# Taking out the small weight loads that TensorE ran behind VectorE, and pairing the evictions of a weight merge

## The chip, the cores and the metric

One Trainium2 chip, all 8 cores. Each core runs the same program on one batch element of 2048 positions and 1024 features, and no data passes between cores. The metric is the device time of the slowest core in microseconds.

## The reference, cut to what matters

Two layers on x of shape (8, 2048, 1024):

```python
x = x + minGRU(layernorm(x))            # gates by sigmoid, a scan over time, layernorm, residual
h = layernorm(x) @ fakequant8(W_fc).T + 2 * lora   # 1024 -> 4096
x = x + (gelu(h) @ fakequant8(W_proj).T + 2 * lora)  # 4096 -> 1024
# layer 1
xk, xv, xr = blends of layernorm(x) with itself shifted by one position
k, v, sr = xk @ Wk.T, xv @ Wv.T, sigmoid(xr @ Wr.T)
x = x + (sr * wkv(w, u, k, v)) @ Wo.T   # wkv: a running weighted mean over time
x = x + tanh(layernorm(x) @ W @ A1 @ A2 + bias)
```

`fakequant8` scales a weight by its largest magnitude over 127, rounds it and scales it back. The kernel folds the low-rank part into the rounded weight.

## The kernel before

Activations lie with features on the 128 partitions (8 groups, `kk` or `m`) and positions along the free dimension (2048, in tiles of 512, or in two halves `th` of 1024). The program is written stage by stage with small bodies, `k.T` for TensorE, `k.V` for VectorE, `k.S` for ScalarE, `k.G` for GpSimd and `k.Y` for the SyncE queue. `k.dep` notes what a body has to wait for, and `body` writes those waits in front of it. Every engine works through its bodies in the order in which the Python code emits them, so a wait in front of one body holds back all later bodies of that engine.

`warm()` emits a TensorE body of two weight loads of the tile `ONESB`, whose result nothing uses. In front of it stands a wait for the newest VectorE mark at that place in the program. It is called at eight places.

The stages that the change touches, in order:

1. **Combine.** `cmb` forms the new residual for 8 groups by 4 tiles, with `warm()` after each tile. Then come `ln_stats` (VectorE casts and squares, TensorE sums over partitions) and `xh2_v`/`xh2_g`, the normalised input of the feed-forward part, with `warm()` after each of six groups.
2. **Rounding W_fc.** `pass2(WFCT, ...)` takes 32 chunks of 128x1024. `qv` is four VectorE instructions a chunk, and `warm()` follows each. Only after all 32 does the code emit the merges: `merge_chunk(..., "s")`, for each half chunk one small matmul (`asl` by `bgr`, the low-rank part), one by the identity `IDN`, and the ScalarE body `mev` that copies the sum over the rounded weight. The low-rank operand comes in by `aring`, two slots loaded by GpSimd's queue. The banks go round over four.
3. **Rounding W_proj.** `pass2(WPRT, ...)`, again 32 chunks of `qv` with `warm()` after each, reading through `ring2` and writing into the tile `H`.
4. **Feed-forward.** Four position tiles `tt`. In each, `mfc` (8 groups `g` of 32 matmuls, read out by the ScalarE body `efc` with GELU), then `mpr` (2 groups of 128 matmuls) and `epr`. For `tt == 0` the merges of W_proj stand between the two: `merge_chunk(..., "v")` with the matmul body `abm2` and the VectorE body `mev2`. So `mfc` of the first tile is emitted after all `warm()` calls of step 3, and `mpr` after all `mev2`.
5. **Blends and wkv.** For each half `th`: eight blends (`bl_g` on GpSimd, `bl_v` on VectorE) with `warm()` after each. Then for each group `m`: `mkv` (32 matmuls for k and v into banks a to a+3), `mr` (16 matmuls for r into banks b and b+1, b = 4 - a, a alternating 0 and 4), `ev1a` and `ev1b` (ScalarE, two exponentials of k), `warm()`, `ev2` (ScalarE, exponential of r), `v1` (VectorE: products, two scans, numerator and denominator), `warm()`, `sdiv` (ScalarE: logarithm and exponential), `v2` (VectorE, last product), `warm()`. `EKBp` and `EKUp` have two buffers each; `EWB`, `EKV` and `DEN` have one.
6. **Output projection.** `mwo` (16 matmuls), `awo` on VectorE, with residual tiles coming in by `x2ring` and going out by `owr`, both on the SyncE queue.
7. **Last part.** `ln_stream_stats`, then `xh4` for 16 tiles (two halves `h2` of 8 groups; every fourth on GpSimd) with `warm()` after each. Then `mm1` (16 matmuls, two banks) and `em1` (VectorE) for 2 halves by 8 groups, and `mm2` and `mm3` in the same way.

Of the kernel before, what the change touches and what calls it, by code (L numbers as in the profile page):

```python
# [8 lines left out]
AF = mybir.ActivationFunctionType  # L9
# [122 lines left out]
def _ap(t):  # L132
    return t if isinstance(t, bass.AP) else t[:]


def bc16(t):
    return _ap(t).bitcast(BF16)
# [6 lines left out]
def tmax(*toks):  # L144
    at = {}
    for t in toks:
        if t is None:
            continue
        if isinstance(t, dict):
            for p, v in t.items():  # L150
                at[p] = max(at.get(p, 0), v)
        else:
            at[t[0]] = max(at.get(t[0], 0), t[1])
    return at
# [27 lines left out]
def build(T=2048, debug=False):  # L182
# [33 lines left out]
    XB0 = nc.alloc_sbuf_tensor("XB0", [128, 8 * RT], BF16)  # L216
# [7 lines left out]
    ONESB = nc.alloc_sbuf_tensor("ONESB", [128, 128], BF16)  # L224
# [16 lines left out]
    PB = [nc.alloc_psum_tensor(f"PB{i}", [128, NSZ], F32) for i in range(8)]  # L241

    with nc.Block() as blk:
        k = K(nc, blk)
# [14 lines left out]
        def bank_wait(ctx, idxs):  # L259
            for i in idxs:  # L260
                if banks[i] is not None:
                    ctx.wait(*banks[i])

        WRHS = bc16(_ap(XB0))[:, 0:512]

        def warm():
            at = {"vector": k.ch["vector"].val}
            k.dep(["tensor"], at=at)
            def wf(t):
                t.ldweights(ONESB[:])  # L270
                t.ldweights(ONESB[:])
            k.T(wf)

        def gdma(wn, out, in_, gate=None, **kw):
            c = k.ch["gd_" + wn]
# [424 lines left out]
        for m in range(8):  # L700
            for n in range(NT):
                sl = slice(n * NSZ, (n + 1) * NSZ)
                if m < 6:
                    sch = "spx%d%d" % (2 * (m // 2), 2 * (m // 2) + 1)
                    slot, tok = xring.load(ci, SP1[m * 128:(m + 1) * 128, sl],
                                           gates=[(sch, 32)])
                else:
                    slot, tok = Xr[m][:, sl], None
                eng = "vector" if ci % 4 != 3 else "gpsimd"
                if eng == "vector":  # L710
                    k.dep([eng], at=tmax(lnh_rows, scan_done[m], tok))
                    def cmb(e, m=m, sl=sl, slot=slot):
                        tmp = SCR[2]
                        e.tensor_sub(tmp[:], HD[m][:, sl], EX[0][:, sl])
                        e.chain()
                        e.tensor_mul(tmp[:], tmp[:], EX[1][:, sl])
                        e.chain()
                        e.tensor_scalar(tmp[:], tmp[:], SM[:, 16 + m:17 + m],
                                        SM[:, 24 + m:25 + m], OP.mult, OP.add)
                        e.chain()  # L720
                        e.tensor_add(tmp[:], tmp[:], XBF[m][:, sl])
                        e.chain()
                        e.tensor_add(Hr[m][:, sl], tmp[:], slot)
                        comb_done[(m, n)] = (eng, e.mark())
                    k.V(cmb)
                else:
                    k.dep([eng], at=tmax(lnh_rows, scan_done[m], tok))
                    def cmb_g1(e, m=m, sl=sl):
                        tmp = SCR[3]
                        e.tensor_sub(tmp[:], HD[m][:, sl], EX[0][:, sl])  # L730
                        e.chain()
                        e.tensor_mul(tmp[:], tmp[:], EX[1][:, sl])
                        e.mark()
                    k.G(cmb_g1)
                    k.dep(["vector"], ["gpsimd"])
                    def cmb_s(e, m=m):
                        e.tensor_scalar(SCR[3][:], SCR[3][:],
                                        SM[:, 16 + m:17 + m],
                                        SM[:, 24 + m:25 + m],
                                        OP.mult, OP.add)  # L740
                        e.mark()
                    k.V(cmb_s)
                    k.dep(["gpsimd"], ["vector"])
                    def cmb_g2(e, m=m, n=n, sl=sl, slot=slot):
                        tmp = SCR[3]
                        e.tensor_add(tmp[:], tmp[:], XBF[m][:, sl])
                        e.chain()
                        e.tensor_add(Hr[m][:, sl], tmp[:], slot)
                        comb_done[(m, n)] = ("gpsimd", e.mark())
                    k.G(cmb_g2)  # L750
                if m < 6:
                    xring.release(ci, comb_done[(m, n)])
                    ci += 1
                warm()
        comb_m = {m: tmax(*(comb_done[(m, n)] for n in range(NT)))
                  for m in range(8)}

# [11 lines left out]
        ln2_rows = ln_stats(lambda kk, n: Hr[kk][:, n * NSZ:(n + 1) * NSZ],  # L769
                            lambda kk, n: comb_done[(kk, n)], EX[0], EX[1])  # L770
        xh2_tok = {}
        for kk in (0, 1, 2, 4, 5, 6):
            k.dep(["vector"], at=tmax(ln2_rows) if kk == 0 else None)
            def xh2_v(v, kk=kk):
                for n in range(NT):
                    sl = slice(n * NSZ, (n + 1) * NSZ)
                    v.tensor_sub(SCR[2][:], Hr[kk][:, sl], EX[0][:, sl])
                    v.chain()
                    v.tensor_mul(XBF[kk][:, sl], SCR[2][:], EX[1][:, sl])
                    v.chain()  # L780
                xh2_tok[kk] = ("vector", k.ch["vector"].val)
            k.V(xh2_v)
            warm()
        k.dep(["gpsimd"], at=tmax(ln2_rows))
        def xh2_g(g):
            for kk in (3, 7):
                for n in range(NT):
# [50 lines left out]
                     ["ar0", "ar1"], issue_eng="gpsimd")  # L838
        ali = [0]

        def merge_chunk(kk, c, dst, bs_ap, a_hbm, qv_tok, first, evac,
                        bs_tok, merged):
            asl, atok = aring.load(ali[0],
                                   a_hbm[0:16, kk * 128:(kk + 1) * 128])
            for h in range(2):
                b = abk[0] % 4
                abk[0] += 1
                dgr = dst(kk, c)[:, h * 512:(h + 1) * 512]
                bgr = bs_ap[0:16, c * 1024 + h * 512:c * 1024 + (h + 1) * 512]
                at = tmax(qv_tok, atok,  # L850
                          *([bs_tok, ("gd_idn", 16)] if first[0] else []))
                first[0] = False
                if evac == "s":
                    k.dep(["tensor"], at=at)
                    def abm(t, b=b, dgr=dgr, bgr=bgr, asl=asl):
                        bank_wait(t, [b])
                        t.matmul(PB[b][:], asl, bgr, start=True, stop=False)
                        t.matmul(PB[b][:], IDN[:], dgr, start=False,
                                 stop=True)
                        t.mark()  # L860
                    k.T(abm)
                    k.dep(["scalar"], ["tensor"])
                    def mev(s, b=b, dgr=dgr):
                        s.activation(dgr, PB[b][:], AF.Copy)
                        banks[b] = ("scalar", s.mark())
                    k.S(mev)
                    merged[(kk, 2 * c + h)] = ("scalar", k.snap("scalar"))
                else:
                    k.dep(["tensor"], at=at)
                    def abm2(t, b=b, bgr=bgr, asl=asl):  # L870
                        bank_wait(t, [b])
                        t.matmul(PB[b][:], asl, bgr, start=True, stop=True)
                        t.mark()
                    k.T(abm2)
                    k.dep(["vector"], ["tensor"])
                    def mev2(v, b=b, dgr=dgr):
                        v.scalar_tensor_tensor(dgr, PB[b][:], 1.0,
                                               dgr, OP.mult, OP.add)
                        banks[b] = ("vector", v.mark())
                    k.V(mev2)  # L880
                    merged[(kk, 2 * c + h)] = ("vector", k.snap("vector"))
            aring.release(ali[0], ("tensor", k.snap("tensor")))
            ali[0] += 1

        def pass2(hbm, order, dst, gates, qtok, qcol, ring, ring_i0, iq,
                  deferred):
            for i, (kk, c) in enumerate(order):
# [19 lines left out]
                qv_tok = ("vector", k.snap("vector"))  # L907
                ring.release(ring_i0 + i, qv_tok)
                deferred.append((kk, c, qv_tok))
                warm()  # L910

        fcm_ready = {}
        fc_first = [True]
# [177 lines left out]
        for th in range(2):  # L1091
            hsl = slice(th * TH, (th + 1) * TH)
            for kk in range(KT):
# [42 lines left out]
                btok = ("vector", k.snap("vector"))  # L1136
                qring.release(kk % 2, btok)
                xhb_free[kk % 2] = btok
                warm()
            blends_done = ("vector", k.snap("vector"))  # L1140

            for m in range(8):
# [51 lines left out]
                    for i in range(NHH):  # L1194
                        banks[a + i] = tok
                k.S(ev1b)
                warm()
                eku_tok = ("scalar", k.snap("scalar"))
                k.dep(["scalar"], at=tmax(rh_done[(th, m)], prev(v1_done, 1)))
                def ev2(s, m=m, b=b):  # L1200
# [49 lines left out]
                                           OP.add, OP.mult)  # L1250
                    v1_done[(th, m)] = ("vector", v.mark())
                k.V(v1)
                warm()
                k.dep(["scalar"], at=tmax(v1_done[(th, m)]))
                def sdiv(s):
                    s.activation(EWB[:], EKV[:], AF.Ln)
# [14 lines left out]
                    g1_done[(th, m)] = tok  # L1271
                    rw_done[(th, m)] = tok
                k.V(v2)
                warm()

        mloop_v = ("vector", k.snap("vector"))
        mloop_s = ("scalar", k.snap("scalar"))
# [99 lines left out]
        for h2 in range(NCH):  # L1377
            for kk in range(KT):
# [12 lines left out]
                qring.release(li4, tok2)  # L1391
                xh4_tok[(kk, h2)] = tok2
                li4 += 1
                warm()

        def h1_sl(kk):
            return bc16(Hf[kk // 2])[:, (kk % 2) * T:(kk % 2) * T + T]
# [200 lines left out]
```

How the kernel before makes its waits and increments, by code:

```python
    def mark(self):  # L47
        K = self._K
        c = K.ch[self._n]
        assert self.last is not None, "mark with no pending instruction"
        self.last.then_inc(c.sem, 1)
        c.val += 1
        self.last = None
        return c.val
# [1 line left out]
    def chain(self):  # L56
        v = self.mark()
        self._e.wait_ge(self._K.ch[self._n].sem, v)
# [1 line left out]
    def wait(self, name, val):  # L60
        if val > 0:
            self._e.wait_ge(self._K.ch[name].sem, val)
# [1 line left out]
    def dma(self, name, out, in_, **kw):  # L64
        K = self._K
        c = K.ch[name]
        ins = self._e.dma_start(out=out, in_=in_, **kw)
        ins.then_inc(c.sem, 16)
        c.val += 16
        self.last = None
        return c.val
# [34 lines left out]
        def run(eng):  # L106
            ctx = Eng(self, eng, name)
            pend = self.pend[name]
            own = self.ch[name]
            if own.val > pend.get(name, 0):
                pend[name] = own.val
            if pend:
                for p, v in sorted(pend.items()):
                    if v > 0:
                        eng.wait_ge(self.ch[p].sem, v)
                pend.clear()
            fn(ctx)
            if ctx.last is not None:
                ctx.mark()
# [159 lines left out]
            def f(g):  # L279
                ins = g.dma_start(out=out, in_=in_, **kw)
                ins.then_inc(c.sem, 16)
                g.last = None
# [1255 lines left out]
        def fin(y):  # L1538
            for name, v in sorted(fin_vals.items()):
                if v > 0:
                    y.wait_ge(k.ch[name].sem, v)
```

## Time and profile before

| | us |
|---|---|
| runs shown, timed | 3179.94 and 3232.47, median 3206.21 |
| the profiled execution | 3165.46 |
| its span on the slowest core (core 7) | 3163.9 |
| spans of the eight cores | 3129.1 to 3163.9 |
| TensorE matmul busy | 1348.0 (43%) |
| VectorE busy | 1461.9 (46%) |
| ScalarE busy | 653.1 (21%) |

No engine is busy for even half of the span. The time is made of stages with different limits, and of waits between engines. So the busy shares are read stage by stage, and each stage's rows for what ended the idle time. A row of the timeline gives the start and the duration in us, the engine, the operation with output<-input, and in brackets the idle time before it with what ended it. PEld is TensorE's weight load.

### The profile page before, as it was taken

Reading aid. Unit: us, or ns where it says so; the run is one execution under the profiler, and the core shown is the slowest. Engines: PE = TensorE matmul, PEld = TensorE weight load, DVE = VectorE, ACT = ScalarE, POOL = GpSimd, SP = SyncE. Lnnn points to the kernel's source line nnn. Section 1 sums busy time; section 2 is a strip of 40 time slices with the busy share of each in tenths; the row PEclk is TensorE's granted clock in tenths of the full one; section 3 lists DMA queues with packets and bytes.
Section 4 is the critical chain, followed back from the end, with each engine's and each line's share of the span. In section 5 each row is a group of like instructions: output and inputs, shape, how many; then the busy total and the mean of one; then the engine's idle time right before and its main releaser. Section 6 shows DMA issues by size and latency. Waiting matters only on the chain.

```text
span 3163.9 us, 19191 instructions; the slowest of 8 cores (3129.1 to 3163.9 us)
## 1 busy us (share of the span) xinstructions
PE 1348.0 (43%) x4868; PEld 509.3 (16%) x5232; DVE 1461.9 (46%) x1702; ACT 653.1 (21%) x754; POOL 274.7 (9%) x219
## 2 busy tenths in 40 slices
PE   3054433040005387797976311433043345240885
PEld 0021110000001132333332000111011111000332
DVE  3866668888999813100101376233824321006322
ACT  0033320000009540223130001233032310070013
POOL 0300000303001001000000024000400000041000
PEclk9987765555555586999988555776566676655998
DMA  7223320400333200201104711000100024652015
GB/s 174 80 89 122 120 82 24 144 32 2 106 108 108 96 1 2 53 21 34 38 17 84 158 50 36 0 0 0 40 0 0 0 50 94 119 150 87 13 42 165
DMA packets 73846, 201.00 MB, mean 64 GB/s; under 512 B 9440, under 2 KB 9440, under 8 KB 70928
## 3 DMA queue, kind: packets, MB, share of 16 engines
q1 hardware_dynamic: 59952, 165.76, 17.3%
q0 software_dynamic: 11776, 19.34, 4.2%
q10 hardware_dynamic: 2016, 14.68, 1.2%
q8 instruction: 47, 0.77, 0.1%
q14 instruction: 55, 0.45, 0.1%
HBM read 179.24 MB, written 39.85 MB: 69 GB/s over the span
## 4 chain that ended last, share of the span: by engine, by line
DVE 34%; PE 28%; DMA 17%; ACT 9%; issue 8%; POOL 2%; SPq 1%; DVEq 1%; ACTq 0%; PEld 0%; POOLq 0%; PEldq 0%
PE PB L38 28%; DVE X L38 9%; DVE SC L38 8%; DMA SC<-SP 7%; DVE E L38 7%; DMA E<-SP 4%; DVE AT L38 4%; ACT L38 4%; DVE XB L38 3%; DVE H L38 2%; DMA E<-WPRT 2%; DVE MX L38 2%; ACT SC L38 2%; ACT X L38 2%; DMA SMT<-SM 1%
## 5 line engine op out<-in xcount | busy, mean ns | idle before, releaser
L38 ACT ACT_TABLE_LOAD x249 | 319.5, 1283 | 2494.5 <-PE PB L38 1190.6
L38 PE MATMUL PB<-XB,X 128*128 128x512 bf16 x1280 | 292.9, 387 | 179.4 <-PE L38 119.0
L38 PE MATMUL PB<-X,H 128*128 128x512 bf16 x512 | 153.7, 473 | 491.1 <-PE L38 491.1
L38 PE MATMUL PB<-XB,H 128*128 128x512 bf16 x896 | 230.1, 416 | 262.2 <-DVE X L38 145.8
L38 PE MATMUL PB<-E,H 128*128 128x512 bf16 x1152 | 279.6, 408 | 63.1 <-DVE X L38 44.7
L38 DVE TENSOR_SCALAR AT<-PB,QS,SMT 128x512 f32<-128x512 f32 x32 | 25.9, 810 | 468.7 <-PE PB L38 342.9
L38 PE MATMUL PB<-SC,ONESB 128*128 128x512 bf16 x256 | 129.5, 608 | 167.7 <-DVE SC L38 145.4
L38 PEld LDWEIGHTS <-ONESB 128*128 128x128 bf16 x364 | 27.2, 103 | 994.7 <-issue 994.7
L38 PE MATMUL PB<-E,ASL 16*128 16x512 bf16 x64 | 37.1, 580 | 291.9 <-DVE AT L38 243.3
L38 PEld LDWEIGHTS PB<-XB,X 128*128 128x128 bf16 x1280 | 123.8, 99 | 229.8 <-issue 95.1
L38 PEld LDWEIGHTS PB<-E,H 128*128 128x128 bf16 x1152 | 118.3, 104 | 224.4 <-issue 108.6
L38 PEld LDWEIGHTS PB<-XB,H 128*128 128x128 bf16 x896 | 90.2, 105 | 382.2 <-issue 305.6
L38 DVE TENSOR_SCALAR SC<-E,DRV 128x1024 f32<-128x1024 f32 x16 | 12.1, 753 | 296.1 <-ACT SC L38 296.1
L38 PE MATMUL PB<-H,X 128*128 128x512 bf16 x512 | 120.8, 391 | 30.3 <-ACT X L38 20.8
L38 DVE TENSOR_TENSOR X<-PB,SC 128x512 f32<-128x512 f32 x32 | 22.1, 692 | 185.9 <-DMA SC<-SP 178.7
L38 ACT ACTIVATE E<-PB,SMT,QS 128x512 bf16<-128x512 f32 x128 | 89.2, 777 | 0.4
L38 POOL TENSOR_TENSOR E<-E 128x1024 f32<-128x1024 f32 x28 | 78.7, 2812 | 94.6 <-DMA E<-SP 92.1
L38 DVE SCALAR_TENSOR_TENSOR H<-PB,H 128x512 bf16<-128x512 f32 x64 | 44.3, 692 | 89.0 <-PE PB L38 88.5
L38 PE MATMUL PB<-MX,SC 1*128 1x1 f32 x4 | 1.1, 343 | 195.8 <-DVE SC L38 195.8
L38 DVE CAST H<-PB 128x512 bf16<-128x512 f32 x64 | 41.2, 686 | 90.7 <-PE PB L38 90.7
L38 PEld LDWEIGHTS PB<-X,H 128*128 128x128 bf16 x512 | 58.5, 116 | 98.7 <-issue 65.7
L38 DVE RECIPROCAL E<-SC 128x512 f32<-128x512 f32 x20 | 67.0, 3352 | 2.4 <-DVE SC L38 0.5
(137 smaller groups left out, 1919.4 us busy)
## 6 DMA issues: line engine op xcount, KB each, us to landing
AT<-WFCT SPq DMA_DIRECT2D x32, 512.0 KB, 3.4
E<-WFCT SPq DMA_DIRECT2D x32, 512.0 KB, 3.4
SC<-WPRT SPq DMA_DIRECT2D x32, 512.0 KB, 3.3
SC<-SP SPq DMA_DIRECT2D x64, 256.0 KB, 3.6
E<-SP SPq DMA_DIRECT2D x56, 256.0 KB, 4.2
AT<-SP SPq DMA_DIRECT2D x24, 512.0 KB, 3.7
E<-SP SPq DMA_DIRECT2D x24, 512.0 KB, 3.7
X<-XT SPq DMA_DIRECT2D x2, 4096.0 KB, 30.0
```

What stands on the lines that cost most here:

```text
L38: ins = f(*args, **kw)
```

## The change

The function `warm` and all its calls are gone, eight call sites in the code. The six bodies of `xh2_v` become one. In `merge_chunk` with `"s"` the ScalarE body is emitted once for both halves of a chunk: it waits for both halves' matmuls, does the two copies, and frees both banks with one mark. All else is as before: each engine's other bodies stand in the same order.

```diff
-        def warm():
-            at = {"vector": k.ch["vector"].val}
-            k.dep(["tensor"], at=at)
-            def wf(t):
-                t.ldweights(ONESB[:])
-                t.ldweights(ONESB[:])
-            k.T(wf)
...
@@ combine @@
                     xring.release(ci, comb_done[(m, n)])
                     ci += 1
-                warm()
...
@@ xh2 @@
-        for kk in (0, 1, 2, 4, 5, 6):
-            k.dep(["vector"], at=tmax(ln2_rows) if kk == 0 else None)
-            def xh2_v(v, kk=kk):
+        k.dep(["vector", "gpsimd"], at=tmax(ln2_rows))
+        def xh2_v(v):
+            for kk in (0, 1, 2, 4, 5, 6):
...
-            k.V(xh2_v)
-            warm()
-        k.dep(["gpsimd"], at=tmax(ln2_rows))
+        k.V(xh2_v)
...
@@ merge_chunk @@
-                    k.dep(["scalar"], ["tensor"])
-                    def mev(s, b=b, dgr=dgr):
-                        s.activation(dgr, PB[b][:], AF.Copy)
-                        banks[b] = ("scalar", s.mark())
-                    k.S(mev)
-                    merged[(kk, 2 * c + h)] = ("scalar", k.snap("scalar"))
+                    sgr.append((b, dgr, kk, 2 * c + h))
+                    if h == 1:
+                        k.dep(["scalar"], ["tensor"])
+                        def mev(s, pair=tuple(sgr)):
+                            for b2, d2, _, _ in pair:
+                                s.activation(d2, PB[b2][:], AF.Copy)
+                            tok = ("scalar", s.mark())
+                            for b2, _, _, _ in pair:
+                                banks[b2] = tok
+                        k.S(mev)
+                        stok = ("scalar", k.snap("scalar"))
+                        for _, _, kk2, g2 in sgr:
+                            merged[(kk2, g2)] = stok
+                        del sgr[:]
...
@@ pass2, after each chunk @@
                 deferred.append((kk, c, qv_tok))
-                warm()
...
@@ blends @@
                 xhb_free[kk % 2] = btok
-                warm()
...
@@ wkv, in the loop over m @@
                 k.S(ev1b)
-                warm()
...
                 k.V(v1)
-                warm()
...
                 k.V(v2)
-                warm()
...
@@ xh4 @@
                 li4 += 1
-                warm()
```

## Rows read from the trace of the kernel before

**Rows 1.** Page, the chain that ended last, share of the span by engine.
```profile
DVE 34%; PE 28%; DMA 17%; ACT 9%; issue 8%; POOL 2%; SPq 1%; DVEq 1%; ACTq 0%; PEld 0%; POOLq 0%; PEldq 0%
```

**Rows 2.** Windows: stretch, length, busy and count per engine, granted clock, DMA share, GB/s.
```profile
785.50:942.90 157.40, 0.00 (x0) 4.73 (x64) 143.57 (x128) 7.42 (x4) 2.05 (x4) 0.50 0.32 108
942.90:1100.70 157.80, 71.61 (x128) 17.83 (x192) 143.57 (x129) 120.34 (x128) 16.96 (x32) 0.50 0.31 103
...
1295.00:1760.00 465.00, 347.97 (x1531) 150.49 (x1529) 40.55 (x54) 97.67 (x120) 5.99 (x8) 0.89 0.21 44
...
2930.00:3160.00 230.00, 179.26 (x767) 72.92 (x765) 63.03 (x96) 40.79 (x48) 4.00 (x2) 0.95 0.23 69
```

**Rows 3.** Timeline, end of rounding W_fc, first merge.
```profile
943.02 0.15 PEld L38 LDWEIGHTS <-ONESB 128*128 128x128 bf16 x2 [4.82 <-issue]
...
943.77 0.58 PE L38 MATMUL PB<-E,ASL 16*128 16x512 bf16 x1 [239.85 <-DVE AT L38]
```

**Rows 4.** Timeline, ScalarE during the merges of W_fc, two later half chunks.
```profile
1064.30 1.28 ACT L38 ACT_TABLE_LOAD   x1
...
1065.60 0.60 ACT L38 ACTIVATE X<-PB 128x512 bf16<-128x512 f32 x1
...
1066.33 1.28 ACT L38 ACT_TABLE_LOAD   x1
```

**Rows 5.** Timeline, end of rounding W_proj, first feed-forward tile, its merges.
```profile
1100.72 0.15 PEld L38 LDWEIGHTS <-ONESB 128*128 128x128 bf16 x2 [4.77 <-issue]
...
1101.64 4.78 PE L38 MATMUL PB<-XB,X 128*128 128x512 bf16 x11 [34.19 <-PE L38]
...
1157.36 7.07 PE L38 MATMUL PB<-XB,X 128*128 128x512 bf16 x32 [0.57 <-PE PB L38]
...
1165.34 3.08 DVE L38 SCALAR_TENSOR_TENSOR H<-PB,H 128x512 bf16<-128x512 f32 x4 [64.73 <-PE PB L38]
```

**Rows 6.** Timeline, wkv loop, one group m from its `v1` on.
```profile
2098.12 0.75 DVE L38 TENSOR_SCALAR SC<-E,DRV 128x1024 f32<-128x1024 f32 x1 [18.48 <-ACT SC L38]
...
2100.17 4.47 DVE L38 TENSOR_TENSOR_SCAN X<-SC,X 128x1024 f32<-128x1024 f32 x2
...
2109.21 1.28 ACT L38 ACT_TABLE_LOAD   x1 [11.27 <-DVE X L38]
...
2112.88 1.23 DVE L38 TENSOR_TENSOR XB<-X,SC 128x1024 bf16<-128x1024 f32 x1 [3.75 <-ACT SC L38]
...
2115.05 9.48 PE L38 MATMUL PB<-X,H 128*128 128x512 bf16 x32 [20.85 <-PE L38]
...
2124.67 1.28 ACT L38 ACT_TABLE_LOAD   x1 [11.96 <-PE PB L38]
```

**Rows 7.** Waits, first half of the wkv loop: total us, times, longest us.
```profile
ACT L38 <- PE PB L38: 176.8, 8, 92.2
```

**Rows 8.** Timeline, first stage (165 to 470 us), VectorE's scan beside matmuls.
```profile
190.69 4.42 DVE L38 TENSOR_TENSOR_SCAN H<-X 128x2048 f32<-128x2048 f32 x1
193.08 3.61 PE L38 MATMUL PB<-XB,H 128*128 128x512 bf16 x16 [0.37 <-PE PB L38]
```

**Rows 9.** Timeline, start of the output projection, and a later matmul group after a pause.
```profile
2559.74 0.32 SPq L67 DMA_DIRECT2D SC<-SP  x1
...
2568.22 0.69 DVE L38 TENSOR_TENSOR X<-PB,SC 128x512 f32<-128x512 f32 x1 [7.16 <-PE PB L38]
...
2587.75 5.21 PE L38 MATMUL PB<-XB,H 128*128 128x512 bf16 x16 [8.61 <-DVE X L38]
```

**Rows 10.** Page, DMA issues: queue, count, KB each, median us to landing.
```profile
SC<-SP SPq DMA_DIRECT2D x64, 256.0 KB, 3.6
```

**Rows 11.** Timeline, end of the last normalisation and start of the last part.
```profile
2926.68 1.23 DVE L38 TENSOR_TENSOR XB<-AT,E 128x1024 bf16<-128x1024 f32 x1
...
2938.67 3.61 PE L38 MATMUL PB<-XB,X 128*128 128x512 bf16 x16 [0.37 <-PE PB L38]
```

**Rows 12.** Timeline, `xh2`: the same product beside GpSimd's products.
```profile
734.63 1.56 DVE L38 TENSOR_TENSOR XB<-SC,E 128x512 bf16<-128x512 f32 x1
```

More of the change, by code:

```diff
@@ L262, in bank_wait @@
                     ctx.wait(*banks[i])
-        WRHS = bc16(_ap(XB0))[:, 0:512]
-        def warm():
-            at = {"vector": k.ch["vector"].val}
-            k.dep(["tensor"], at=at)
-            def wf(t):
-                t.ldweights(ONESB[:])
-                t.ldweights(ONESB[:])
-            k.T(wf)
         def gdma(wn, out, in_, gate=None, **kw):
@@ L839, in build @@
         ali = [0]
+        sgr = []
         def merge_chunk(kk, c, dst, bs_ap, a_hbm, qv_tok, first, evac,
```

## The prediction

> **What bounds the kernel now.** I read the page first: by its busy shares (in the table above) no engine is busy for half the span, and the chain that ended last passes through VectorE, TensorE, transfers and ScalarE in turn [rows 1]. The limit is therefore order. I then took the windows by stage and, at every place where `warm()` stands, the timeline, asking one question: what stands behind this wait in TensorE's queue, and was it ready earlier?
>
> Three stretches show the answer. While W_fc is rounded, VectorE is busy 143.57 of 157.40 us and TensorE runs nothing but the 64 idle loads; while W_proj is rounded, VectorE is busy just as long, and TensorE only does the merges [rows 2]. Then VectorE idles for 64.73 us while TensorE does the first feed-forward tile [rows 5]. The first merge matmul starts at 943.77, right behind the last idle load of the W_fc rounding, although the first chunk was rounded some 150 us before [rows 3]. The first feed-forward matmul starts at 1101.64, behind the last idle load of the W_proj rounding [rows 5], although it needs no W_proj.
>
> In the wkv loop one turn is a closed ring: matmuls of k and v, exponentials, `v1`, `sdiv`, `v2`, and only then, behind the third `warm()`, the next matmuls [rows 6]. Nothing overlaps there.
>
> **The change, part by part.** The matmuls keep their order; what goes is the wait for VectorE in front of them.
>
> *A. Feed-forward, first tile.* VectorE has one unbroken queue here: 32 chunks of W_fc and 32 of W_proj, 785.5 to 1100.6 [rows 2, 5]. The change takes nothing from it. What moves is TensorE's work beneath it. One chunk is rounded every 4.92 us (157.4/32). A merge needs per chunk four small matmuls and two ScalarE copies. On ScalarE a half chunk took 2.02 us, of which 1.28 is a table load, once per body [rows 4]. Paired, a chunk takes about 1.28 + 2 x 0.60 + 0.1 = 2.6 us in place of 4.0, and either is below 4.92. So the merges keep up with the rounding and end about 7 us after the last chunk, near 950. The pairing saves 32 table loads, 41 us of ScalarE time, at no gain on the path: the rounding covers it. Without that cover it would be worth up to 32 x 1.4 = 45 us.
>
> `mfc` of the first tile then runs from about 950 for as long as now, 1101.64 to about 1164.5, 63 us. It ends near 1013, under the W_proj rounding. At 1100.6 the first `mev2` finds its banks filled and starts about 0.3 us later, in place of at 1165.34, which had waited 64.73 us [rows 5]. Gain 64.4 us. The merges of W_proj after it are paced by `mev2` and by the loads of `ASL`, and keep their length. What is late next is those same merges: the loss of the whole overlap would give back 64.4, and that is the far bound of this term. The near bound is 0 loss: there are 88 us of slack (1101 - 1013).
>
> *B. The wkv loop.* In the new order, `mkv` of group m+1 needs its banks: b and b+1 are freed by `ev2` of m, and b+2 and b+3 were freed by `v1` of m-1. So it starts about when `v1` of m does. From there, `v1` lasts 11.1 us (2098.12 to 2109.2), `sdiv` until about 2112.7, thus 14.6 us [rows 6]. `mkv` needs 9.5 [rows 6] and `mr`, 16 matmuls at full rate, 0.4 + 3.6 [rows 8], together 13.5, and `mkv` is what `ev1a` needs. So `ev1a` of m+1 finds its input ready and follows `sdiv` in ScalarE's queue after about 0.1 us. Before, ScalarE idled 11.96 us there, waiting for TensorE [rows 6]. Of the 16 turns, 14 follow another turn; the two first of a half wait for the blends as before. In the first half the wait came 8 times for 176.8 us, of which the first was 92.2, so the other seven had 12.09 each [rows 7]. Gain 14 x (12.09 - 0.1) = 168 us. The turn goes from 34.3 to about 22.4: `v1` 11.1, `sdiv` 3.5, the three exponential bodies the rest, and `v2` (1.23) lies under the exponentials.
>
> What is late next is ScalarE and VectorE, in series; TensorE has about 8.7 us to spare. Its clock: the matmuls of a turn begin at 1.2 GHz (the 32 take 9.48 [rows 6], where 32 at 2.4 GHz took 7.07 [rows 5]). A pause of 8.61 us elsewhere was also followed by a slow start, 5.21 for 16 in place of 3.61 [rows 8, 9], so I take the same slow start. If all 48 ran at 1.2 GHz, at 4.78/11 = 0.43 us each [rows 5], `mkv` would end after 13.8, still in time, and `mr` after 21.0, where `ev2` wants it at 22.4 less its own 2.5 (a table load of 1.28 and two copies of 0.60, as in [rows 4]), 19.9. That costs 1.1 a turn, 16 us in all: the far bound.
>
> Does VectorE slow down when TensorE works beside it? Two scans of 1024 with TensorE idle took 4.47 [rows 6], one scan of 2048 beside matmuls at full rate 4.42 [rows 8]. I take 0.
>
> *C. Output projection.* The first two `mwo` run under the last `v1`. `awo` then waits for the first residual tile, issued at 2559.74. Such a transfer lands 3.6 us after its issue in the median [rows 10], so it starts near 2563.5 in place of 2568.22 [rows 9]: 4.7 us, bounds 0 and 7.2 (the whole wait on TensorE). After it the stage goes at the pace of its transfers, as now.
>
> *D. Last part.* `mm1` of the first two groups runs under the second half of `xh4`. The third needs a bank that `em1` frees. `em1` can begin when VectorE's last `xh4` ends (2926.68 + 1.23), so the third group starts near 2929.5 in place of 2938.67 [rows 11]. It starts slow, 1.6 us more [rows 8, 9]. Gain 7.6 us, bounds 0 and 9.
>
> *E. The rest.* The combine, `xh2` and the blends are paced by VectorE and GpSimd, and nothing useful stood behind the waits there. The idle loads in front of the first matmuls of a half took under 1 us each: 1 us in all. Joining the `xh2` bodies saves nothing that counts.
>
> **Two rules weighed.** The granted clock is 0.50, the level of 1.2 GHz, while only the 64 idle loads run [rows 2], so they hold nothing up, and the turn's matmuls start slow right behind them [rows 6]. The Trainium skill, "TensorE: Matmul & The Clock Gate", "Why this matters for your kernels", asks that TensorE have no idle gaps, since the clock falls back in them. If the idle loads counted as work for it, taking them out would cost; by the rows it costs nothing, and I go by the rows. Second, the wait in front of an idle load did hold the merges [rows 3]. The same page ("Step-by-step: what each phase is for") says that only weight loads are pulled ahead, and matmuls keep program order; had the merges been able to pass the waiting loads, the change would do nothing. The trace agrees with the page.
>
> **Sum.** 64.4 + 168 + 4.7 + 7.6 + 1 = 245.7, or 246 us. The profiled execution took 3165.5, so the same kind of execution would take 2920. The runs shown lie higher, 3179.94 and 3232.47. I take off the sum from 3179.94, the middle one of the three times: 2934 us. Against the median of the two runs shown, 3206, the sum would give 2960.
>
> **Rivals.**
> - *TensorE late in the wkv loop:* all its matmuls there at 1.2 GHz, 16 us back, 2950. For it: the slow starts. Against: the clock rose within every burst. Chance 0.05.
> - *A does not come:* something else holds the first feed-forward tile to the end of the W_proj rounding, for example a merge paced below the rounding. 2934 + 64 = 2998. Against: both paces above. Chance 0.03.
> - *B does not come:* another wait closes the ring, of a bank or of a single buffer. 2934 + 168 = 3102. I find none in the code. Chance 0.03.
> - *Contention:* VectorE slows beside TensorE as it does beside GpSimd, where a product of 128x512 took 1.56 [rows 12] in place of 0.69 ([rows 9] has an addition of that size). On the 11 us of `v1` that would add up to 14 us a turn, 196 in all, 3130. Against: the scans. Chance 0.02.
> - *The change does nothing:* 3180. Against: the waits in [rows 3, 5]. Chance 0.02.
> - *Slower: the clock.* The idle loads keep the clock ready in a way that the granted clock does not show, and without them long bursts stay at 1.2 GHz. In the feed-forward stretch from 1295 to 1760, 1531 matmuls took 348 us and would take 658 at 0.43 each; in the last part, 767 took 179 and would take 330 [rows 2, 5]. Together 461 lost against 246 won: 2934 + 461 = 3395. It decides once 53% of these matmuls stay slow. Against: the clock is 0.50 with the loads [rows 2], and the feed-forward stretch, at 0.89, has none in it. Chance 0.02.
>
> My forecast keeps 0.83.
>
> **How the numbers follow.** 2934 is the likeliest case. Upward the range takes in the late TensorE, the higher starting time (3232 - 246 = 2986) and the loss of A: 3000. Downward it takes the lowest starting time (2920) and 25 us for terms B to D being under-counted: 2895. Faster by over 2% (below 3142; about what a measurement of this kernel can tell from no change) are the forecast and the first four rivals, with 0.95 after rounding down; within 2% the case of no effect, 0.03; slower 0.02.
>
> **What would show each step.** A: merge matmuls among the rounding from 790 on, feed-forward matmuls before 1100, and no VectorE pause of 64 us. B: about 22.4 us between one `v1` and the next, and ScalarE without its 12 us wait on TensorE. If instead the wait stays and names a bank, B is wrong; if `v1` grows beyond 11.1, it is contention; if ScalarE waits on TensorE for `ev2`, it is the clock. C and D: first `awo` and third `mm1` 4 to 9 us sooner against the end of the stage before. The clock: if the steady 7.1 us per 32 matmuls of the feed-forward tiles rises, the slow rival holds.

## The result, and the profile after

The changed kernel takes 2919 us where the kernel before took 3164 (medians of the comparison's runs); the ratio is 0.9214, with a 95% interval of 0.9187 to 0.9242. Some executions of either kernel take some per cent longer, with a lower granted clock on one die, and the ratios leave them out. The runs of before came out lower in this comparison than in the two shown earlier, so the 2934 that was forecast is 15 us high, while the saving, 245 us between the medians, is the 246 of the sum. In the two profiled executions the spans are 3163.9 and 2916.6 us: 247.3 less.

The page after, in the same order as before: busy time by engine, and the chain that ended last.

```profile
PE 1350.7 (46%) x4868; PEld 483.4 (17%) x4868; DVE 1463.9 (50%) x1702; ACT 609.0 (21%) x722; POOL 273.9 (9%) x219
...
DVE 37%; PE 23%; DMA 19%; ACT 9%; issue 8%; POOL 1%; SPq 1%; DVEq 1%; ACTq 0%; POOLq 0%
```

TensorE and VectorE do the same work in the same time as before: 4868 matmuls and 1350 us, 1702 instructions and 1464 us. 364 weight loads are gone, and 32 ScalarE table loads. TensorE's share of the chain fell from 28% to 23% [rows 1]. The time came out of waiting.

**The feed-forward part.** Windows of core 5 of the changed kernel, in the columns of [rows 2]: rounding W_fc, rounding W_proj, merges of W_proj.

```profile
788.10:945.30 157.20, 69.38 (x124) 12.55 (x124) 142.33 (x127) 80.36 (x97) 17.09 (x35) 0.50 0.34 109
945.30:1104.80 159.50, 62.11 (x264) 25.61 (x264) 144.90 (x130) 35.46 (x45) 1.45 (x3) 0.69 0.32 101
1104.80:1171.30 66.50, 34.78 (x60) 5.97 (x60) 44.17 (x64) 0.00 (x0) 13.56 (x28) 0.50 0.03 2
```

VectorE is as busy as before in both roundings. TensorE now does the merges in the first and the first feed-forward tile in the second. Timeline of the same kernel: the first merge, the first feed-forward matmuls, the last 32 of that first tile, the last rounding instruction and the first `mev2`.

```profile
797.85 0.58 PE L38 MATMUL PB<-E,ASL 16*128 16x512 bf16 x1 [91.07 <-ACT E L38]
...
952.26 8.06 PE L38 MATMUL PB<-XB,X 128*128 128x512 bf16 x29 [2.71 <-ACT X L38]
...
1007.44 7.07 PE L38 MATMUL PB<-XB,X 128*128 128x512 bf16 x32 [0.57 <-PE PB L38]
...
1103.37 1.23 DVE L38 SCALAR_TENSOR_TENSOR H<-SC,AT 128x1024 bf16<-128x1024 f32 x1
1104.69 7.85 DVE L38 SCALAR_TENSOR_TENSOR H<-PB,H 128x512 bf16<-128x512 f32 x10
```

The merge starts 9.7 us after the rounding of its chunk began (788.17), released by ScalarE, which had scaled its low-rank operand. The first feed-forward matmul starts at 952.26, and the first tile ends at 1014.5. The first `mev2` follows the last rounding instruction after 0.09 us, where it waited 64.73 us before [rows 5].

**The wkv loop.** Timeline of one turn, from `v1` to the next `v1`, to be laid beside [rows 6].

```profile
2007.14 0.75 DVE L38 TENSOR_SCALAR SC<-E,DRV 128x1024 f32<-128x1024 f32 x1 [6.83 <-ACT SC L38]
2007.46 8.47 PE L38 MATMUL PB<-X,H 128*128 128x512 bf16 x32 [9.06 <-ACT SC L38]
...
2009.19 4.47 DVE L38 TENSOR_TENSOR_SCAN X<-SC,X 128x1024 f32<-128x1024 f32 x2
...
2016.29 3.61 PE L38 MATMUL PB<-XB,H 128*128 128x512 bf16 x16 [0.37 <-PE PB L38]
...
2017.90 1.28 ACT L38 ACT_TABLE_LOAD   x1 [10.94 <-DVE X L38]
...
2021.58 1.22 DVE L38 TENSOR_TENSOR XB<-X,SC 128x1024 bf16<-128x1024 f32 x1 [3.75 <-ACT SC L38]
2021.59 1.28 ACT L38 ACT_TABLE_LOAD   x1 [0.18 <-ACT SC L38]
...
2024.05 1.28 ACT L38 ACT_TABLE_LOAD   x1
...
2026.80 1.28 ACT L38 ACT_TABLE_LOAD   x1 [0.19 <-ACT X L38]
...
2029.35 0.75 DVE L38 TENSOR_SCALAR SC<-E,DRV 128x1024 f32<-128x1024 f32 x1 [6.55 <-ACT SC L38]
```

The matmuls of the next group start 0.3 us after `v1`, released by ScalarE (`ev2`, which frees their banks), and end at 2015.9 for k and v, before the ScalarE body that reads them starts at 2021.6, and at 2019.9 for r, before its body starts at 2026.8. The exponentials follow the end of `sdiv` at once: 0.18 us of idle time where it had been 11.96 [rows 6]. The turn is 22.2 us (2029.35 - 2007.14). Over all 14 turns that follow another turn, the mean from one `v1` to the next is 22.2 us, where it was 34.2. The scans take 4.47 us with matmuls beside them, as without. The clock still starts low: 32 matmuls took 8.47 us where 7.07 is full rate [rows 5].

**Output projection and last part.** The first `awo`, and then the third and fourth `mm1`, to be laid beside [rows 9] and [rows 11].

```profile
2329.16 0.69 DVE L38 TENSOR_TENSOR X<-PB,SC 128x512 f32<-128x512 f32 x1 [2.00 <-DMA SC<-SP]
```

```profile
2685.68 5.52 PE L38 MATMUL PB<-XB,X 128*128 128x512 bf16 x16 [18.14 <-DVE H L38]
2691.57 3.61 PE L38 MATMUL PB<-XB,X 128*128 128x512 bf16 x16 [0.37 <-PE PB L38]
```

The first `awo` now waits 2.00 us, for its residual tile, and no longer for TensorE. The third `mm1` starts 1.7 us after the last `xh4` of VectorE (which ends at 2684.03), with a slow start: 5.52 us for 16 matmuls in place of 3.61.

**Where the 247 us went,** between the same marks in both timelines:

| stretch | before | after | difference | forecast |
|---|---|---|---|---|
| start to first rounding | 785.6 | 788.2 | +2.6 | 0 |
| first rounding to first `mev2` | 379.7 | 316.5 | -63.2 | -64.4 |
| first `mev2` to first wkv matmul | 778.6 | 773.4 | -5.2 | -1 |
| wkv loops, to the end of the last `v2` | 617.1 | 449.1 | -168.0 | -168 |
| last `v2` to first `awo` | 7.2 | 2.0 | -5.2 | -4.7 |
| first `awo` to the last `xh4` of VectorE | 359.7 | 354.9 | -4.8 | 0 |
| last `xh4` to the fourth `mm1` | 14.7 | 7.5 | -7.2 | -7.6 |
| fourth `mm1` to the end | 221.3 | 225.0 | +3.8 | 0 |

The four stretches with a forecast of 0 or -1 moved by -5 to +4 us, -3.6 in all. Their causes were not traced. Moves of this size can't be told from the spread between executions: in the traces of the experiments below whose code up to there is that of the changed kernel, the first rounding starts anywhere from 780.8 to 793.4 us.

### The profile page after: what moved, and what is told of

Its sections match the earlier page's. It is cut to its first block, busy times and chain, and to the rows that moved or that the text cites. A ratio compares the mean times of both kernels' runs of the same rounds, so it can differ in the third digit from the quotient of the medians.

```text
span 2916.6 us, 18362 instructions; the slowest of 8 cores (2889.4 to 2916.6 us)
## 1 busy us (share of the span) xinstructions
PE 1350.7 (46%) x4868; PEld 483.4 (17%) x4868; DVE 1463.9 (50%) x1702; ACT 609.0 (21%) x722; POOL 273.9 (9%) x219
## 4 chain that ended last, share of the span: by engine, by line
DVE 37%; PE 23%; DMA 19%; ACT 9%; issue 8%; POOL 1%; SPq 1%; DVEq 1%; ACTq 0%; POOLq 0%
PE PB L38 23%; DVE SC L38 9%; DVE X L38 9%; DMA SC<-SP 7%; DVE E L38 7%; DVE AT L38 4%; ACT L38 4%; DMA E<-SP 4%; DVE XB L38 3%; DVE H L38 3%; DMA E<-WPRT 2%; DVE MX L38 2%; ACT SC L38 2%; ACT X L38 2%; DMA SMT<-SM 1%
## 5 line engine op out<-in xcount | busy, mean ns | idle before, releaser
L38 PE MATMUL PB<-E,H 128*128 128x512 bf16 x1152 | 279.0, 408 | 63.2 <-DVE X L38 44.6
L38 PE MATMUL PB<-SC,ASL 16*128 16x512 bf16 x64 | 36.5, 570 | 118.7 <-DVE H L38 90.3
L38 PE MATMUL PB<-XB,ONESB 128*128 128x512 bf16 x64 | 32.4, 608 | 78.8 <-POOL XB L38 45.8
```

The costliest lines, as they stand in the source:

```text
L38: ins = f(*args, **kw)
```

## The experiments

Each ratio is to the kernel before on the same chip, which took 3167 to 3178 us (median) there. All kernels but the first start from the changed one, 2919 us.

### The loads stay, the wait goes

```diff
         def warm():
-            at = {"vector": k.ch["vector"].val}
-            k.dep(["tensor"], at=at)
             def wf(t):
```

> The kernel before with the wait for VectorE taken out of warm(), and nothing else: all 364 idle weight loads stay, and the merges stay unpaired. Theory (only the wait cost time): the whole gain is there, about 2920 us, ratio near 0.922, within 10 us of the changed kernel; the loads themselves cost at most 364 x 0.15 = 55 us of TensorE time, nearly all beside other work, so at most some 5 us. Rival (the loads themselves held the matmuls up, or the pairing carried the gain): 3000 us or more. Second rival (loads do hold the clock up once they no longer block): granted clock above 0.50 while W_fc is rounded.

Measured: 2926.0 us, ratio 0.9224 (0.9187 to 0.9261), against 0.9214 for the change itself. While W_fc is rounded, the window shows the merges, and the clock at 0.50:

```profile
788.00:945.00 157.00, 69.34 (x124) 12.66 (x124) 143.01 (x129) 122.73 (x127) 17.07 (x35) 0.50 0.37 109
```

So two deleted lines are the change. The 364 loads, the unpaired merges and the six separate `xh2_v` bodies cost nothing that this measures. This is the cleanest test: no other instruction differs from the kernel before. In the wkv loop the 32 matmuls start slow here too, with idle loads in front of them that wait for nothing:

```profile
1982.81 9.10 PE L38 MATMUL PB<-X,H 128*128 128x512 bf16 x32 [8.27 <-ACT SC L38]
```

### One wait back in the wkv loop

```diff
                 k.V(v1)
+                warm()          # first run; in the second run it stands behind k.V(v2)
```

> The changed kernel with warm() put back only behind v1 in the wkv loop. Theory: the next k and v matmuls start at the end of v1 (11.1 us after its start) plus about 0.9, take 9.5, so that ev1a starts about 21.6 us after v1's start in place of 14.7: turns of about 29.1 in place of 22.2, 14 x 6.9 = 97 us more, near 3016. Rival (any wait of TensorE on VectorE closes the ring as a whole): turns of 34.3, near 3087. Rival (this one never mattered): 22.2, near 2919.

> The changed kernel with warm() put back only behind v2 in the wkv loop. Theory: this one wait closes the ring, turns of 34.2 us in place of 22.2, 14 x 12 = 168 us more, and the first projection tile 5 us later: near 3092. Rival (the three waits add up): clearly less, 3000 to 3060.

Measured: 3015 us behind `v1` (a second run 3031), ratio 0.9531 (0.9475 to 0.9587), and 3083 us behind `v2` (a second run 3155), where 3092 was expected. The traces are those of the 3031 and the 3083. Waits of ScalarE in the first half, of the run behind `v1` and then of the one behind `v2` (total, times, longest):

```profile
ACT L38 <- PE PB L38: 40.7, 6, 7.5
```

```profile
ACT L38 <- PE PB L38: 72.9, 6, 12.3
```

Per turn that is 6.8 and 12.15 us, against 6.9 and 12 expected. The turns, from scan to scan over seven turns, are (2092.72 - 1891.69)/7 = 28.7 us and (2135.46 - 1896.16)/7 = 34.2. The wait behind `v2` alone brings back the whole ring, the one behind `v1` a bit over half. So the costs of several waits do not add up: each costs what it holds back. The trace of the run behind `v2` also has the late start of the projection again, with the first `awo` 7.2 us after the last `v2` (2.0 in the changed kernel):

```profile
2497.61 0.69 DVE L38 TENSOR_TENSOR X<-PB,SC 128x512 f32<-128x512 f32 x1 [7.17 <-PE PB L38]
```

### One wait back in the rounding of W_proj

```diff
                 deferred.append((kk, c, qv_tok))
+                if hbm is WPRT:
+                    warm()
```

> The changed kernel with warm() put back only behind each chunk of W_proj's rounding. Theory: the first feed-forward tile waits for the end of the rounding again, VectorE idles 64 us before mev2, 63 us more, near 2982. Rival (what held the tile was the late merges of W_fc, not this wait): near 2919.

Measured: 2988.3 us, ratio 0.942 (0.9384 to 0.9457). Timeline: the first feed-forward matmuls and the first `mev2`.

```profile
1106.81 3.46 PE L38 MATMUL PB<-XB,X 128*128 128x512 bf16 x9 [156.05 <-PE L38]
...
1169.65 3.10 DVE L38 SCALAR_TENSOR_TENSOR H<-PB,H 128x512 bf16<-128x512 f32 x4 [63.87 <-PE PB L38]
```

The 64 us are back, with all merges done long before: 156 us of TensorE's idle time lie in front of the tile. So this wait held it, not late merges.

### The waits back in the rounding of W_fc, with the pairing and without

```diff
                 deferred.append((kk, c, qv_tok))
+                if hbm is WFCT:
+                    warm()
```

> The changed kernel with warm() put back only behind each chunk of W_fc's rounding, merges paired. Theory: all merges run after the rounding, at the pace of TensorE or ScalarE, about 3 us a chunk, 32 x 3 = 95 us, so the first feed-forward tile starts near 1042 and ends near 1105, just where VectorE is done with W_proj: 0 to 5 us more, 2919 to 2924. Rival (late merges are late on the path): 30 us or more.

> The same, with the merges' evictions unpaired as in the kernel before. Theory: 64 bodies of 2.02 us make 129 us, the first feed-forward tile starts near 1075 and ends near 1138, 33 us after VectorE: near 2952. So the pairing is worth some 30 us where its cover is gone. Rival (pairing never matters): same time as the paired one.

Measured: 2934.4 us paired, 2959.9 us unpaired. The first `mev2` of the paired run, and then of the unpaired one:

```profile
1114.25 3.08 DVE L38 SCALAR_TENSOR_TENSOR H<-PB,H 128x512 bf16<-128x512 f32 x4 [12.38 <-PE PB L38]
```

```profile
1139.52 3.10 DVE L38 SCALAR_TENSOR_TENSOR H<-PB,H 128x512 bf16<-128x512 f32 x4 [36.60 <-PE PB L38]
```

The paired case missed its bound: 12.4 us of idle VectorE time and 15 us more between the medians (11 by the ratios, 0.925 against 0.9214), where at most 5 were expected. From the first merge to the first feed-forward matmul it took 106 us (944.6 to 1050.4), not 95, and the waits of that stretch name a part of the reason, the loads of the low-rank operand:

```profile
PE PB L38 <- DMA ASL<-AFC: 10.7, 9, 1.5
```

The unpaired case came as expected: 36.6 us late. The difference, 24 us in the traces and 26 by the ratios, is what the pairing is worth once the rounding no longer covers the merges.

### The pairing undone

The ScalarE body of `merge_chunk` as before the change, one per half chunk; nothing else.

> The changed kernel with the merges' evictions unpaired as before. Theory: a half chunk of 2.02 us, 4.04 a chunk, still keeps up with the 4.92 of the rounding, 32 more table loads of 1.28 us on ScalarE, no time lost: 2919, within 5 us. Rival (unpaired merges delay the first tile): 10 us or more.

Measured: 2922.6 us, ratio 0.9217 (0.9188 to 0.9245), the same as the change to well within the interval. First `mev2`: no idle time in front of it.

```profile
1106.26 9.45 DVE L38 SCALAR_TENSOR_TENSOR H<-PB,H 128x512 bf16<-128x512 f32 x12
```

### The waits back behind `xh4`

```diff
                 li4 += 1
+                warm()
```

> The changed kernel with warm() put back only behind each tile of xh4. Theory: the first two matmul groups of the last part move back behind the normalisation, 7 us more, near 2926. Rival: nothing, because the time between the last xh4 and the end grew by 4 us elsewhere in the changed kernel and that came with the early groups: 2919 to 2922.

Measured: 2931.8 us, ratio 0.9232 (0.9189 to 0.9274). The trace has the fourth `mm1` at 2701.03, 15.6 us after the last `xh4` of VectorE (2684.23 + 1.22), against 7.5 in the changed kernel: 8 us. The 12.7 us between the medians is more, but the two intervals overlap almost wholly, so only the 8 us of the trace can be called shown. From the last `xh4` of VectorE to the end, runs without this wait took from 229.5 to 261.6 us, so neither the rest of the 12.7 nor the idea that the early groups give 4 us back later can be decided here.

### Filling TensorE's pause in the wkv loop

```diff
                     rh_done[(th, m)] = ("tensor", t.mark())
+                    for _ in range(60):             # first run
+                        t.ldweights(ONESB[:])
+                    bank_wait(t, [b + NHH])         # second run, both except in the last group
+                    for _ in range(24):
+                        t.matmul(PB[b + NHH][:], wr_sl(0, m), xr_sl(0)[:, 0:512],
+                                 start=True, stop=True)
```

> The changed kernel with 60 more idle weight loads of ONESB behind the matmuls of r in every turn of the wkv loop, waiting for nothing. They fill about 6 us of TensorE's pause of some 9 us a turn. Theory (weight loads do not hold the granted clock up): the k and v matmuls of the next turn still start at 1.2 GHz (8.5 to 10 us for the 32), the granted clock of the loop stays at 0.75 to 0.79, the time stays at 2919 within 10. Rival, the one by which the idle loads were worth having: the 32 take 7.1 us, clock above 0.9; the time is the same in that case too, because TensorE is not late in the loop.

> The same with 24 matmuls of 128x512 in place of the 60 loads (results overwritten by the next group). Theory: matmuls do hold the clock up, the 32 k and v matmuls take about 7.1 us, granted clock of the loop above 0.9, time still 2919 within 10, since scans, logarithm and exponentials set the turn. Rival: clock as without filler. If the turn of 22.2 us shrinks with the faster matmuls, the reading that TensorE is off the path falls.

Measured: 2927.5 us with loads (0.918 to 0.9289) and 2917.0 us with matmuls (0.9151 to 0.9252), both the time of the change; turns of 22.2 us in both. Windows over six turns of the first half: the changed kernel, the one with loads, the one with matmuls.

```profile
1920.00:2053.00 133.00, 74.10 (x285) 29.44 (x283) 69.07 (x78) 64.11 (x72) 0.00 (x0) 0.81 0.00 0
```

```profile
1912.00:2045.00 133.00, 76.24 (x282) 44.91 (x644) 69.05 (x79) 64.09 (x72) 0.00 (x0) 0.78 0.00 1
```

```profile
1907.00:2040.00 133.00, 101.83 (x406) 41.72 (x404) 69.05 (x78) 64.09 (x72) 0.00 (x0) 0.87 0.00 0
```

With 28 us more TensorE work in these six turns, 4.6 a turn, the time did not move: TensorE is off the path in the loop. About the clock the runs say less than was hoped. The loads ran at 0.04 us each ((44.91 - 29.44)/361), so 60 of them filled about 2.5 us of the pause and not 6; the clock did not rise (0.78 against 0.81), and the next matmuls still started slow. With matmuls the clock went to 0.87, not above 0.9, and the expectation of 7.1 us for 32 matmuls failed:

```profile
1972.52 8.75 PE L38 MATMUL PB<-X,H 128*128 128x512 bf16 x32 [3.27 <-ACT SC L38]
...
1995.02 9.59 PE L38 MATMUL PB<-X,H 128*128 128x512 bf16 x32 [4.59 <-ACT SC L38]
```

After the pauses of 3.3 and 4.6 us that remained, the 32 matmuls still started slow. Whether weight loads would hold the clock if they filled the whole pause is open.

### Following the ring further: one ScalarE body a turn

Bodies `sdiv` of group m-1, `ev1a`, `ev1b` and `ev2` of group m joined, with the waits for the matmuls inside. `v2` of group m-1 is emitted behind it. No arithmetic changes.

```diff
+                def evs(s, ...):
+                    s.activation(EWB[:], EKV[:], AF.Ln)            # group m-1
+                    s.chain()
+                    s.activation(DEN[:], EWB[:], AF.Exp, scale=-1.0)
+                    div_tok.append(("scalar", s.mark()))
+                    s.wait(*kv_done[(th, m)])
+                    ...                                            # ev1a, ev1b
+                    s.wait(*rh_done[(th, m)])
+                    ...                                            # ev2
```

> The changed kernel with the turn's four ScalarE bodies made one: logarithm and exponential of the group before, then the exponentials of this group, waits inside. Theory (the ring is now v1 plus ScalarE's queue, and a table load stands in front of each body): three loads of 1.28 us less a turn, turns of 18.4 in place of 22.2, 14 x 3.8 + 2 x 2.6 = 58 us less, near 2861. Rival (TensorE becomes late: its matmuls start at v1's start and need 13.5 to 14 us, ev1a would want them after 14.6): less than 40 us of gain, ScalarE waiting for TensorE. Rival (the loads stay although the bodies are joined): 2919.

Measured: ratio 0.9006 (0.8973 to 0.9039), 2852 us at the 3167 of the kernel before beside it, so 66 us below the change by the ratios (0.9214 - 0.9006, times 3167). Timeline of one turn's ScalarE part, and the next `v1`:

```profile
1992.80 1.28 ACT L38 ACT_TABLE_LOAD   x1 [10.94 <-DVE X L38]
1994.10 1.06 ACT L38 ACTIVATE SC<-X 128x1024 f32<-128x1024 f32 x1
1995.25 1.06 ACT L38 ACTIVATE SC<-SC 128x1024 f32<-128x1024 f32 x1
1996.45 1.09 ACT L38 ACTIVATE X<-PB 128x512 f32<-128x512 f32 x2
...
1997.42 1.27 ACT L38 ACTIVATE X<-PB,SMT 128x512 f32<-128x512 f32 x2
1998.56 1.10 ACT L38 ACTIVATE SC<-PB 128x512 bf16<-128x512 f32 x2
1999.84 0.75 DVE L38 TENSOR_SCALAR SC<-E,DRV 128x1024 f32<-128x1024 f32 x1 [2.14 <-ACT SC L38]
```

One load in place of four; the whole kernel has 171 in place of 217, and 46 is 14 x 3 + 2 x 2. The turn is (2001.89 - 1895.08)/6 = 17.8 us where 18.4 was expected: the three loads make 3.84 of the 4.4 us, and the rest lies in the gaps between the bodies. ScalarE does not wait for TensorE. This confirms the account of the ring after the change: `v1` and ScalarE's queue in series.

### The stores of the output projection on another queue

On top of that, `owr` of the output projection issued by ScalarE in place of SyncE, and the ring slots 2 and 3 freed by `v2`.

```diff
-                    k.dep(["sync"], at=tmax(vtok))
+                    k.dep(["scalar"], at=tmax(vtok))
...
-                    k.Y(owr)
+                    k.S(owr)
```

> The same, and the stores of the output projection issued from ScalarE's queue in place of SyncE's, so that a residual load no longer stands behind the store of the tile before (the third and fourth load slot are freed by v2, where they were freed by GpSimd). Theory (the stage goes at one transfer's latency a tile, 5.7 us, because the loads are serial): four loads in flight, 3 to 3.5 us a tile, 182 us become 100 to 110, near 2785. Rival (the 16 DMA engines are the limit there): under 30 us of gain, VectorE still waiting 4 us for each load.

Measured: 2735.0 us, ratio 0.8631 (0.8588 to 0.8674), by the ratios 119 us below the one before it, more than the 67 expected (2852 to 2785). Windows over the projection, first with the stores on SyncE, where it lasts on past the window, then on ScalarE:

```profile
2267.00:2440.00 173.00, 79.46 (x224) 27.85 (x224) 20.06 (x29) 0.00 (x0) 3.04 (x4) 0.71 0.44 102
```

```profile
2267.00:2329.00 62.00, 50.41 (x213) 20.46 (x214) 19.91 (x30) 0.00 (x0) 0.00 (x0) 0.94 0.95 227
```

30 additions of VectorE in 62 us in place of 29 in 173. From its first addition to its last the stage takes 68 us, where it took 191, and not the 100 to 110 that were expected. It went at one transfer's latency at a time: VectorE waited 143 us for residual loads in the first window. Now its waits are mostly for stores (36 us of 46), and the 16 DMA engines are busy for 95% and move 227 GB/s, where they were at 44%; so it is most likely the DMA engines that bound it. The two edits, the queue of the stores and the two slots, were not run apart, so their shares are not shown.

## Why the prediction was right

- **What stands behind the wait.** The step that carried it was to list, for each `warm()`, the TensorE work behind it and when that work was ready. The first run shows that the wait alone is the gain, and the runs with waits put back at one place show that terms A, B and D sit where they were put. The waits of the combine, of `xh2` and of the blends, forecast at 1 us together, were not put back by themselves.
- **Term A, 64.4:** 63.2 between the marks, and 64 to 69 us in the run with the W_proj waits. The slack was 1104.7 - 1014.5 = 90 us, where 88 was worked out.
- **Term B, 168:** 168.0 between the marks, and 167.5 as the sum of the 14 turns. Both halves of the reading were tested: a later start of the matmuls costs by its lateness (28.7 and 34.2 us a turn), and more TensorE work in the pause costs nothing.
- **Term C, 4.7:** 5.2, and the whole of it is back in the run with the wait behind `v2`. **Term D, 7.6:** 7.2, and 8 in the run that undid it.
- **The pairing at no gain:** 3.5 us between the medians, inside the interval. Its worth without cover had been bounded at 45 us; 24 to 26 were measured, since TensorE and the operand loads then pace the merges. The size of that bound was the weaker part.
- **The starting time.** 3179.94 was the middle of three times and 15 us too high. That is the difference between 2934 and 2919; the range took it in.
- **The rivals.** TensorE late in the loop: in the turn shown it ended 5.7 us (k and v) and 6.9 us (r) before ScalarE's bodies that read its results. The 8.7 us that the prediction gave it to spare are 8.9 by its own terms (22.4 - 13.5), and the pause measured 9.06. Contention: the scans took 4.47 us in both. The clock: the steady 7.07 us for 32 matmuls in the feed-forward tiles is unchanged. By the rule of the Trainium skill, "TensorE: Matmul & The Clock Gate", "Why this matters for your kernels", that idle gaps lower the clock, the matmuls should go on starting slow after each pause; the trace agrees (8.47 us in place of 7.07, and 8.75 after a pause of 3.27). But the idle loads had not prevented it, with the wait (9.48, [rows 6]) or without (9.10, first run).

## What to carry to other kernels

Before an instruction that does no work is put into an in-order queue, ask what stands behind its wait. Here two lines of waiting cost 8% of the time, and the loads that they guarded cost nothing. When such a wait goes, work out the new ring at once: it names the next gain, here ScalarE's table loads in the loop, one for each body, and then a queue in which loads stand behind stores.

## What the runs showed of the hardware that was not expected

- A table load of 1.28 us stood in front of each separate ScalarE body, even for exponentials that follow exponentials. With logarithm and exponentials in one body, one load remained of four.
- After a pause of only 3.27 us, 32 matmuls took 8.75 us in place of 7.07.
- Weight loads with nothing to wait for took 0.04 us each, 60 of them 2.46 us.
- With loads and stores on two queues (and two slots freed sooner), the output projection moved 227 GB/s, where the highest slice of the page of before has 174.
